# A kernel of attention and mixture-of-experts layers: each scatter of rows to their slots waits for the one before it

## The reference

```python
idx = top_idx.T.reshape(-1); gat = gates.T.reshape(-1)       # 2 x 2048 choices
pos = jnp.sum(jnp.cumsum(onehot, axis=0) * onehot, axis=-1) - 1
keep = pos < CAPACITY
xe = jnp.zeros((E_ROUTED, CAPACITY, D)).at[idx, pos_c].set(h[tok], mode='drop')
a = jnp.einsum('ecd,edf->ecf', xe, W1); b = jnp.einsum('ecd,edf->ecf', xe, W3)
ye = jnp.einsum('ecf,efd->ecd', jax.nn.silu(a) * b, W2)
routed = zeros.at[tok].add(ye[idx, pos_c] * (gat * keep)[:, None])
shared = jax.nn.silu(h @ W1s) * (h @ W3s) @ W2s
x = x + jnp.tanh(g_ffn[1]) * (routed + shared)
```

## Time and profile before

| | us |
|---|---|
| median of 3 runs | 964.91 (963.47 to 965.41) |
| profiled execution, its own time | 958.46 |
| its span in the trace | 956.7 |
| TensorE busy in the span | 880.3 (92%) |
| POOL busy in the span | 276.3 (29%) |
| mean granted clock of TensorE | 0.975 of full speed |

### The profile page before, as it was taken

One profiled execution on the slowest core, in us unless ns is written; L12 is line 12 of the kernel. 1 busy time (PEld: TensorE's weight loads), 2 busy tenths in 40 slices (PEclk: granted clock), 3 DMA queues, 4 the chain that ended last, 5 costly groups with the idle time before them and its releaser, 6 DMA issues.

```text
span 956.7 us, 17804 instructions
## 1 busy us (share of the span) xinstructions
PE 880.3 (92%) x5836; PEld 799.0 (84%) x5836; DVE 540.8 (57%) x1143; ACT 429.7 (45%) x936; POOL 276.3 (29%) x319
## 2 busy tenths in 40 slices
PE   5979989999969999996679998999999999999996
PEld 3757767999957777875468898999999999999985
DVE  4646755555568767658023556473737363645556
ACT  2535554777746555532022345262616262525330
POOL 4314331777764342045750000102020202020100
PEclk9989999999989999999889999999999999999998
DMA  5522214567620000112211132221314141323152
GB/s 199 160 92 98 79 60 172 157 220 219 191 65 6 6 6 5 13 38 94 87 54 34 34 93 80 94 93 59 110 54 121 62 123 53 115 68 109 48 176 88
DMA packets 74229, 86.93 MB, mean 91 GB/s; under 512 B 30964, under 2 KB 46226, under 8 KB 74060
## 3 DMA queue, kind: packets, MB, share of 16 engines
q1 hardware_dynamic: 70636, 79.86, 26.8%
q0 software_dynamic: 3552, 6.55, 2.0%
HBM read 64.08 MB, written 23.63 MB: 92 GB/s over the span
## 4 chain that ended last, share of the span: by engine, by line
PE 77%; DVE 6%; ACT 3%; another core or an unknown queue 3%; issue 3%; DMA 3%; SPq 3%; POOL 1%; ACTq 0%; DVEq 0%; POOLq 0%
PE score L262 11%; PE score L264 11%; PE score L263 11%; PE bank_p L262 6%; PE bank_p L263 6%; PE bank_p L264 6%; PE bank L558 5%; PE score L538 4%; PE bank_p L549 3%; PE bank L578 3%; PE bank L570 3%; PE bank L504 2%; DMA raw<-w_second_d 2%; SPq L323 1%
## 5 line engine op out<-in xcount | busy, mean ns | idle before, releaser
L1058 ACT ACTIVATE silu<-score 128x366 f32<-128x366 f32 (+1 forms) x144 | 72.6, 504 | 306.7 <-PE score L264 264.8
L1391 DVE TENSOR_TENSOR prod<-silu,score 128x366 f32<-128x366 f32 (+1 forms) x144 | 82.1, 570 | 128.2 <-ACT silu L1058 118.4
L262 PE MATMUL score<-xe_hi,w_hi 128*128 128x366 f32 x448 | 149.9, 335 | 2.7 <-DVE prod L1391 2.7
L1859 POOL DMA_INDIRECT slots_out<-yh,home_of x42 | 40.9, 973 | 377.8 <-DVE yh L1517 377.8
L263 PE MATMUL score<-xe_lo,w_hi 128*128 128x366 f32 x448 | 148.7, 332 | 0.0
L264 PE MATMUL score<-xe_hi,w_lo 128*128 128x366 f32 x448 | 148.7, 332 | 0.0
L262 PE MATMUL bank_p<-w_hi,hid_hi 128*122 128x256 f32 (+1 forms) x464 | 133.4, 288 | 9.7 <-DVE residual L1473 6.2
L263 PE MATMUL bank_p<-w_lo,hid_hi 128*122 128x256 f32 (+1 forms) x464 | 131.8, 284 | 0.0
L264 PE MATMUL bank_p<-w_hi,hid_lo 128*122 128x256 f32 (+1 forms) x464 | 131.6, 284 | 0.0
L262 PE MATMUL score<-act_hi,w_hi 128*128 (+2 forms) x256 | 89.4, 349 | 13.0 <-DVE prod L1391 7.9
L262 PEld LDWEIGHTS bank_p<-w_hi,hid_hi 128*122 128x122 f32 (+1 forms) x464 | 87.4, 188 | 11.3 <-DVE residual L1473 6.4
(11 more groups left out here) (189 smaller groups left out, 1757.0 us busy)
## 6 DMA issues: line engine op xcount, KB each, us to landing
raw<-w_second_d SPq DMA_DIRECT2D x108, 256.0 KB, 2.7
raw<-w_first_d SPq DMA_DIRECT2D x72, 256.0 KB, 3.6
slot_rows<-yh SPq DMA_DIRECT2D x8, 771.0 KB, 3.4
yh<-slot_rows SPq DMA_DIRECT2D x8, 734.9 KB
v_blk<-values SPq DMA_DIRECT2D x256, 5.0 KB, 2.0
slots_out<-yh SPq DMA_DIRECT2D x8, 512.0 KB, 4.4
wa<-attn_w_d SPq DMA_DIRECT2D x8, 256.0 KB, 4.2
yh<-slots_out SPq DMA_DIRECT2D x4, 512.0 KB, 8.1
```

The source lines that it names most:

```text
L262: nc.tensor.matmul(o, a_hi, b_hi, start=start, stop=False)
L1058: nc.scalar.activation(silu[0:rows_n, buf, 0:width], src, ACT.Silu).then_inc(silu_done, 1)
L1391: nc.vector.tensor_tensor(prod[0:rows_n, buf, 0:width], silu[0:rows_n, buf, 0:width], up, ALU.mult).then_inc(gu_free, 1)
L1859: nc.gpsimd.indirect_dma_start(out=ye, out_offset=bass.IndirectOffsetOnAxis(ap=home_of[:, e, j:j + 1], axis=0), in_=y_out[:, j, :], in_off ...
```

## The change

Ahead of every scatter but the first, POOL now waits until all scatters issued so far have landed. The one wait of this kind that was there, at k = 16, is covered by the new one. Nothing else is changed.

```diff
             for k in range(2 * T):
                 t = k % T
+                if k > 0:
+                    pool.wait_ge(scattered, 16 * k)
                 if k == T:
-                    pool.wait_ge(scattered, 16 * T)
                     nc.gpsimd.tensor_copy(yh[:, :, D], home[:, 1, :]).then_inc(home_next, 1)
                     pool.wait_ge(home_next, 2)
                 nc.gpsimd.indirect_dma_start(
```

## The result

The changed kernel takes 986.73 us (median of 6 runs, 986.43 to 990.15); the kernel before took 963.06 in the same comparison (median of 6). The ratio is 1.0263, with a 95% interval of 1.0228 to 1.0298: slower by 2.6%. The forecast was 985.0 us, with 976 to 995 as range.

A forecast was written before the change was run, and what follows sets the result against it. TensorE, carrying 77% of the span, bounds the kernel until it waits for the scattered slots: 20.0 plus 0.1 us on 958.46 gives 978.6, plus the 6.45 offset 985.0, range 976 to 995.

The forecast's parts named there:

- the scatters become the bound: Expert 0's slots, lying ready 35.9 us early, come late; TensorE starts its transposes on them 20.0 us later.
- The period: POOL's scatters: landing plus 0.80 us release to start, 3.1 us each; more than 3.13 or less than 2.9 refutes it.
- The lower bound: Scatter period at least 2.9 us, from a lone last output scatter's 2.17 us landing.
- The lock of the port: Scatters starting inside DVE operations with both inputs in SBUF lengthen; about 5 of 31 pay 0.31 us: 1.6 us.
- The load: SP's load of expert 0's slots: 17.7 us after issue, plus 0.3 for the pieces behind it; upper bound 22.2.
- TensorE's idle time as cover: Recovered 22.9 us become a 20 to 43 us wait for slots; raw-piece wait absorbs 2.4 us of half-pace loss.
- the offset: The shown runs' median, 964.91, stood 6.45 us above the profiled execution; carried over to the forecast.
- The stalls as instruction fetches: In shared chunk 1, "remote" waits, 22.9 us lost, are instruction fetches that get through once scatters have drained; an inference.
- Lasting stalls (999): Rival: stalls last as long as the scatters, TensorE reaches the slots 34 us later, 999 us; chance 0.09.
- The longer period: Rival, upper part of the main case: landing of 2.6 us or more DVE collisions, period 3.4, 9.3 us more, 994.
- Faster: Rival: scatter period 2.0 us, preparation hidden and landing 1.7, gains 16 us, giving 949; chance 0.04.
- nothing to see: Rival: period near 2.5 us, slack and recovered stall just used up, or waits find semaphores full; 965; chance 0.03.

The follow-up runs named there:

- experiments 1: Changed kernel with the wait only ahead of every fourth scatter: 938.11 us against 936.25 for the kernel before, ratio 1.0016.
- experiment 6: The kernel before, unchanged, run again for a trace on another chip: 965.15 us.
- 9 to 11: Changed kernel with waits every fourth scatter (9, 11): 937.48 and 938.29 us; with one or two scatters in the air (10): 940.10; kernel before 936.98, 936.18, 936.98.
- experiment 7: Changed kernel with waits ahead of scatters 1 to 16 only: 960.43 us against 965.32 for the kernel before, ratio 0.9954.
- experiment 2: Changed kernel with each scatter waiting for the one before the last, on two semaphores: 939.18 us against 936.25 for the kernel before, ratio 1.003.
- experiment 3: Changed kernel with POOL's first scatter also waiting until shared chunk 2 is done: 1067.42 us.
- experiment 4: Changed kernel with expert 0's down pieces issued ahead of SP's wait for the scatters: 987.64 us against 936.25 for the kernel before, ratio 1.0558.
- experiment 8: Changed kernel with each scatter sending only the first 64 of 128 rows: 981.1 us in one run.
- burst late (12): Kernel before with all scatters back to back, but only after shared chunk 2: 1003.68 us.
- experiment 5: Changed kernel again, unchanged, on another chip: 987.54 us against 965.32 for the kernel before, ratio 1.0239.

## Why the prediction was right, and where it was lucky

**That the scatters become the bound: shown.** In the kernel after TensorE waits 49.45 us for the slots' load; in experiments 1, 6 and 9 to 11 it does not wait for it. In all variants the end follows the moment at which TensorE begins on the slots. Span less that moment:

| kernel | TensorE starts on the slots | span | difference |
|---|---|---|---|
| before | 549.80 | 956.7 | 406.9 |
| after | 578.95 | 984.8 | 405.9 |
| every fourth (1) | 530.3 | 934.9 | 404.6 |
| two in the air (2) | 532.9 | 938.7 | 405.8 |
| scatters late (3) | 657.6 | 1065.3 | 407.7 |
| pieces first (4) | 577.47 | 985.3 | 407.8 |
| before again (6) | 558.28 | 963.3 | 405.0 |
| waits 1 to 16 (7) | 551.6 | 957.2 | 405.6 |
| 64 rows (8) | 573.4 | 979.3 | 405.9 |
| burst late (12) | 595.1 | 1001.6 | 406.5 |

The repeats (experiments 5 and 9 to 11) have 405.0 to 407.0. The start moves by 127 us, the difference by 3. Within these 3 us everything that the change costs passes through this one moment, and experiment 7 hit it within 1 us by the same sum.

**The period: the mechanism right, the term too small.** I took 3.1 us from two landings, 2.41 and 2.37 us. They belong to scatters 15 and 31, counted from 0, and each of these has only 58 rows with room; they were the only two of the 32 whose landing anything waited for. The full scatters take 3.47. By the prediction's own sign, more than 3.13, this period is refuted. This was the step "nearer to the row of the same instruction": the instruction was the same, the work was not. The lower bound has the same flaw. Its 2.17 us come from the last output scatter, which holds slots 610 to 731 of the last expert; by the reference that expert has 301 rows, so all of these slots are empty, their homes lie out of bounds, and nothing is written. The 31 periods took 557.08 - 452.18 = 104.9 us, where I had 96.1 + 0.3 + 1.6 = 98.0. Of the 6.9 missing, 4.8 are the 13 full periods (13 x 0.37), 1.7 is the first period, 4.80 us, and 1.1 are the six of 3.29; less was lost to DVE than I had booked. The first period was 3.75 where the scatters ran late (experiment 3). What lengthens it, I did not test.

The page "DMA: Bandwidth & Descriptors" of the Trainium skill (section "Anatomy of one DMA — SWDGE (gpsimd) path") fits a DMA issued from GpSimd as 2.0 us plus its bytes over 436 GB/s. As an estimate from that page, 64 rows of 1028 bytes would be 0.15 us. The runs show 0.37 for these scatters of rows.

**The lock of the port: right in kind.** In the kernel after one scatter was stretched (1.44 us, at 505.19) and the copy behind it took 0.52 in place of 0.22, some 0.8 us in all against my 1.6. DVE's hid_lo had begun at 505.09. Of such collisions more appeared in experiment 8, and none in experiment 3, where DVE was idle: there every scatter but the first took 0.97 to 0.99 us.

**The load: 17.7 alone was right, 0.3 for the pieces was not.** It measures 18.0 alone and 19.6 with the pieces. The bound of 22.2 held it.

**TensorE's idle time as cover: right.** It was through with chunk 2 at 529.5, where I had 526.9, and waited 49.45 us, where I had 43. Expert 0's wait for its raw pieces shrank from 4.28 to 2.26 us and took up the half clock at the start, as forecast: the slots moved by 29.15 us and the span by 28.1.

**The lucky part: the offset.** On the profiled executions the change cost 986.66 - 958.46 = 28.2 us, and I had 20.1. I then carried over the 6.45 us by which the median of before stood above its profiled execution. The kernel after had no such offset (986.73 against 986.66; in experiment 5 it was 2.2 us). Varying stalls in chunk 1 may be a reason: the two traces of the kernel before, of executions of 958.46 and 965.15 us, reach the slots at 549.80 and 558.28, and in the kernel after whatever is lost there disappears in the wait for the slots. But that is not shown, since the runs of before also spread over 5 us where it takes 936. Two errors, 8.1 us too little and 6.45 too much, nearly cancel in 985.0 against 986.73. I had carried the offset over without knowing its cause.

**The stalls as instruction fetches: open, and my reading of them weakened.** The kernel before took 963 to 965 us in two comparisons and 936 to 937 in three, each of those three on another chip; the serial version takes 987 on a chip of the slower kind, and with its pieces moved (experiment 4) 988 on one of the faster. Where the kernel before stalls, the waits were seen only with back-to-back scatters in the air or just landed (rows of before, experiments 6 and 7) and never in the serial version (experiment 5). This speaks for the scatters as one condition. But on three chips the times of the kernel before leave no room for stalls, and half of the ten waits in the two stalled traces don't end at a drain. Something that differs between the comparisons is a second condition, perhaps the chip, and no run names it.

The traces also list the packets of instruction queues, and they do not support the reading. In experiment 6 DVE's wait of 10.16 us ends at 468.74. The queues that moved anything between 452.5 and 477.0 (packets, MB, share):

```profile
q0 software_dynamic: 768, 1.98, 22.8%
q1 hardware_dynamic: 442, 0.80, 10.2%
```

So no instruction packet stands in the trace around the end of that wait, and none between 450.5 and 476.0 in the kernel before, where DVE's 11.59 us end at 474.95. The kernel after has one in that time:

```profile
q8 instruction: 1, 0.02, 0.2%
```

In all twelve traces without stalls in chunk 1 a packet of 16 KB on this queue starts between 468 and 473; in the two with them it starts at 481.7 and 491.1. Whether it is late because engines wait, or engines wait because it is late, is not shown; DVE's long waits at least had ended before it. The page "DMA: Bandwidth & Descriptors" of the Trainium skill (section "Queues, rings and completion order") says that each DMA engine takes turns between its queues, packet by packet, by which no fetch should have to wait for a whole burst. The three chips agree with that; the stalling ones do not, if fetches are what waited.

**The rivals.** Lasting stalls (999): out, no remote wait in the kernel after. The longer period: this is what happened, 3.38 us on average, and with it some 8 of the 9 us above my sum that this rival named; only the offset hid it. Faster, or nothing to see: out, since no period of the kernel after came below 3.06 us. They named a mean period of 2.52 as break-even, and experiment 7 happens to have it, (529.34 - 451.08)/31 = 2.52, on a chip with stalls: TensorE began on the slots at 551.6, between the 549.80 and the 558.28 of the two traces of the kernel before. Where the kernel before takes 936, an estimate puts the break-even near (530.3 - 19.6 - 2.4 - 452.6)/31 = 1.8 us: at a pitch of 1.87 in experiment 2 TensorE waited 2.1 us for the slots.

## What to carry to other kernels

A wait added on an engine that nothing waits for is free only until its slack is spent: count the slack from the data's landing to its first use, multiply the new period by the number of issues, and look up who queues behind. When a duration is read from the one row where something waits for it, ask whether that instance did the same work as the others; here two scatters with fewer than half their rows stood for thirty-two. And an offset between a profile and the median has a cause: carry it over only if you know the cause and the change leaves it on the path.

## What the runs showed of the hardware

- The landing of an indirect scatter depends on the rows that it writes: periods of 3.47 us with 128 rows of 1028 bytes, 3.10 with 64 sent and 3.11 with 49 to 82 kept of 128 sent. A waiting engine was let go 2.37 to 2.41 us after the start of a scatter that keeps 58 rows, and 2.17 us after that of one that keeps none. A wait ahead of it adds 0.80 us of preparation that otherwise hides (0.30 us between two).
- The same kernel takes 936 to 937 us on three chips and 963 to 965 in the two other comparisons. In the two traces of the slower kind the loss stands in one loop pass of 34 us of work, in waits for which the trace has no releaser. A comparison of two kernels on one chip, 1.026, is therefore not the ratio on another: with 987 against 936 it was 1.056 (experiment 4, whose end is that of the changed kernel within 1 us).
- After a wait of 49 us TensorE's matmuls of 366 columns took 0.51 us where they take 0.33, at a granted clock of 0.50 (1.2 GHz). It cost little, since expert 0 had a later wait for its weights, which shrank by 2.0 us.
